# Folding 1/smooth into the values of an attention unit: a GpSimd product and one VectorE product per output

## The reference, cut to what matters

```
core = _gqa(q, k, v).reshape(b, s, nh * d)
...
xout = _gqa(qx, kx, vx).reshape(b, s, nh * d)
cat = jnp.concatenate([core, xout], axis=-1)
catq = _div_clamp_fp8(cat, proj_smooth)
return jnp.einsum('bsi,oi->bso', catq, wproj) * (proj_in_scale * proj_w_scale)
```

## Time and profile before

| | before |
|---|---|
| median of 3 runs | 708.38 us (707.12 to 709.31) |
| span of the profiled execution | 708.0 us |
| PE busy | 623.2 us, 88% |
| DVE busy | 552.2 us, 78% |
| ACT busy | 421.1 us, 59% |
| POOL busy | 274.9 us, 39% |
| mean granted TensorE clock | 0.973 |

### The profile page before, as it was taken

The page is one execution under the profiler, slowest core; times in us unless marked ns, Lnnn a source line. Parts: engine busy times, 40 slices in busy tenths (PEclk is TensorE's granted clock), DMA queues, the critical chain, the costliest instruction groups (busy, mean ns, idle before and its releaser), DMA issues.

```text
span 708.0 us, 13489 instructions
## 1 busy us (share of the span) xinstructions
PE 623.2 (88%) x4521; PEld 496.4 (70%) x4567; DVE 552.2 (78%) x1340; ACT 421.1 (59%) x1371; POOL 274.9 (39%) x371
## 2 busy tenths in 40 slices
PE   4347989988889999999999999999899999999946
PEld 3246767766668777777777877777788787786725
DVE  7997778976677857879788669888864677769698
ACT  4246766755677736566856556657665566673631
POOL 3224663442423563433335544333333256341131
PEclk9987999998999999999999999999999999999987
DMA  8255844743472222322234223422343233320001
GB/s 268 68 181 171 305 127 143 221 156 121 110 229 111 97 98 97 98 98 98 98 112 97 98 82 109 101 97 98 98 146 108 67 124 103 98 31 1 0 1 59
DMA packets 38414, 80.09 MB, mean 113 GB/s; under 512 B 3502, under 2 KB 28746, under 8 KB 33610
## 3 DMA queue, kind: packets, MB, share of 16 engines
q1 hardware_dynamic: 38160, 79.21, 35.5%
q10 hardware_dynamic: 186, 0.02, 0.0%
HBM read 66.62 MB, written 12.60 MB: 112 GB/s over the span
## 4 chain that ended last, share of the span: by engine, by line
PE 57%; DVE 27%; issue 5%; ACT 5%; POOL 3%; DMA 2%; SPq 0%; DVEq 0%; ACTq 0%; POOLq 0%
PE bank L588 12%; PE bank L712 12%; PE bank L692 9%; PE bank L595 6%; PE bank L661 4%; PE bank L736 3%; PE bank L678 2%; DVE Cb L1755 2%; DVE nm L1740 2%; POOL rs L1318 2%; PE bank L693 1%; PE bank L726 1%; DMA WH<-wh_split 1%; DVE Cb L1770 1%; DVE Cb L1771 1%
## 5 line engine op out<-in xcount | busy, mean ns | idle before, releaser
L712 PEld LDWEIGHTS bank<-V,Pt 128*128 128x128 f32 x1024 | 126.7, 192 | 39.3 <-DVE Cb L1755 26.8
L712 PE MATMUL bank<-V,Pt 128*128 128x129 f32 x1024 | 138.0, 278 | 10.5 <-DVE Cb L1755 8.9
L1066 ACT ACTIVATE square<-bank 128x128 bf16<-128x128 f32 x372 | 98.1, 276 | 74.8 <-PE bank L588 45.3
L692 PE MATMUL bank<-QT,KTt 128*128 128x512 f32 x256 | 132.7, 600 | 2.7 <-POOL diag L1342 2.4
L1049 ACT ACTIVATE Pt<-bank 128x512 f32<-128x512 f32 x128 | 76.6, 599 | 74.6 <-remote 49.4
L1740 DVE TENSOR_REDUCE nm<-bank 128x2 f32<-128x512 f32 x128 | 82.1, 683 | 35.8 <-PE bank L678 35.7
L1318 POOL TENSOR_TENSOR rs<-ve,mhalf 128x6 f32<-128x6 f32 x64 | 94.7, 1480 | 5.3
L1342 POOL TENSOR_TENSOR diag<-identb,nm 128x512 bf16<-128x512 bf16 x64 | 67.0, 1047 | 67.3 <-DVE nm L1740 67.2
L588 PE MATMUL bank<-WQ,xq 128*128 128x256 f32 x496 | 79.0, 304 | 9.5 <-DMA WH<-wh_split 3.4
L588 PEld LDWEIGHTS bank<-WQ,xq 128*128 128x128 f32 x496 | 67.0, 196 | 21.9 <-DVE nm L1740 12.0
L1755 DVE SCALAR_TENSOR_TENSOR Cb<-bank,ro,ism 128x128 bf16<-128x128 f32 x256 | 78.1, 347 | 4.5
(11 more groups left out here) (241 smaller groups left out, 1117.2 us busy)
## 6 DMA issues: line engine op xcount, KB each, us to landing
WQ<-wq_split SPq DMA_DIRECT2D x29, 1024.0 KB, 7.7
WH<-wh_split SPq DMA_DIRECT2D x29, 384.0 KB, 8.9
ism<-smooth_inverse SPq DMA_DIRECT2D x32, 256.0 KB, 6.4
wq_split<-stage SPq DMA_DIRECT2D x6, 1024.0 KB, 4.6
wst<-in_L_xattn_wproj SPq DMA_DIRECT2D x16, 256.0 KB, 3.8
wh_split<-stageh SPq DMA_DIRECT2D x6, 384.0 KB, 4.4
wst<-in_L_xattn_wq SPq DMA_DIRECT2D x8, 256.0 KB, 4.7
wst<-in_L_xattn_wqx SPq DMA_DIRECT2D x8, 256.0 KB, 4.7
```

What stands on the lines that cost most here:

```text
L692: nc.tensor.matmul(o[:], KTt[u % 2][:, x, t * P:(t + 1) * P], QT[u % 2][:, x, :], start=True, stop=False)
L712: last = nc.tensor.matmul(o[:, h * (P + 2):h * (P + 2) + P + 1], Pt[:, x, k, h * S + t * P:h * S + (t + 1) * P], V[u % 2][:, x, k, 0:P + 1 ...
L1066: last = A(square[:, t, h], head(t, h), ACT.Square, accum_out=ss[:, t, h:h + 1])
```

## The change

ACT now copies the values to a new tile `Vr`. A new POOL function `scaled_values(u)` makes two products, one for each kind x: values of both key tiles, spread over both heads, times 1/smooth of each head, into a `V` that holds a copy for each head (f32, 512 elements for each partition and product). POOL does it for unit u + 1 right after `half(u + 1)`. PE's `weigh` reads the copy of its head, and waits for the new semaphore `v_scaled` before tile 0 of each kind. An output on DVE is then the reciprocal and one product of two over both heads (256 elements). The wait for `ism` goes from DVE to POOL, and SP's `load_smooth` waits for `v_scaled` of the unit two earlier rather than for its last output.

```diff
-        V = [eb(f"V{i}", [P, 2, NT, P + 4]) for i in range(2)]
+        Vr = [eb(f"Vr{i}", [P, 2, NT, P]) for i in range(2)]
+        V = [eb(f"V{i}", [P, 2, NT, HPG, P + 4]) for i in range(2)]
...
                 if u >= 2:
-                    sp.wait_ge(s["o_evac"], 4 * (u - 1))
+                    sp.wait_ge(s["v_scaled"], 2 * (u - 1))
                 sp.dma_start(ism[:, u % 2], smooth_dram.rearrange("(x f) -> x f", x=2)[:, g * HPG * P:(g + 1) * HPG * P]
...
                 pe.wait_ge(s["exp_done"], 4 * u + 2 * x + 2)
+                if t == 0:
+                    pe.wait_ge(s["v_scaled"], 2 * u + x + 1)
...
-                                                Pt[:, x, k, h * S + t * P:h * S + (t + 1) * P], V[u % 2][:, x, k, 0:P + 1],
+                                                Pt[:, x, k, h * S + t * P:h * S + (t + 1) * P], V[u % 2][:, x, k, h, 0:P + 1],
...
                 if u >= 2 and t == 0:
-                    act.wait_ge(s["pv_done"], 4 * (u - 1))
-                A(V[u % 2][:, :, t, 0:P], QB[2 * t + 1][:].rearrange("p (x j c) -> p x j c", x=2, j=2)[:, :, 1, :], ACT.Copy
+                    act.wait_ge(s["v_scaled"], 2 * (u - 1))
+                A(Vr[u % 2][:, :, t, :], QB[2 * t + 1][:].rearrange("p (x j c) -> p x j c", x=2, j=2)[:, :, 1, :], ACT.Copy
...
+            def scaled_values(u):
+
+                pool.wait_ge(s["v_ready"], 2 * (u + 1))
+                pool.wait_ge(s[f"ism{u % 2}_loaded"], 16 * (u // 2 + 1))
+                if u >= 2:
+                    pool.wait_ge(s["pv_done"], 4 * (u - 1))
+                for x in range(2):
+                    gp.tensor_tensor(V[u % 2][:, x, :, :, 0:P], Vr[u % 2][:, x].unsqueeze(2).to_broadcast([P, NT, HPG, P]),
+                                     ism[:, u % 2, x].rearrange("p (h d) -> p h d", h=HPG).unsqueeze(1)
+                                     .to_broadcast([P, NT, HPG, P]), ALU.mult).then_inc(s["v_scaled"], 1)
...
                     half(u + 1)
+                    scaled_values(u + 1)
                 if u == 2:
                     narrow_parts(5)
                 if u == UNITS - 3:
...
-                if x == 0 and t == 0:
-                    dve.wait_ge(s[f"ism{u % 2}_loaded"], 16 * (u // 2 + 1))
-                    if u >= 2:
-                        dve.wait_ge(s["cT2_done"], u - 1)
+                if x == 0 and t == 0 and u >= 2:
+                    dve.wait_ge(s["cT2_done"], u - 1)
...
-                link(v.reciprocal(ro[:, x, t, :], o[:, 0:HPG * (P + 2)].rearrange("p (h c) -> p h c", h=HPG)[:, :, P]))
-                for h in range(HPG):
-                    last = v.scalar_tensor_tensor(out=c4[:, t, x, h, :], in0=o[:, h * (P + 2):h * (P + 2) + P],
-                                                  scalar=ro[:, x, t, h:h + 1], in1=ism[:, u % 2, x, h * P:(h + 1) * P],
-                                                  op0=ALU.mult, op1=ALU.mult)
-                    if h < HPG - 1:
-                        ch.add(last)
-                last.then_inc(s["o_evac"], 1)
+                heads = o[:, 0:HPG * (P + 2)].rearrange("p (h c) -> p h c", h=HPG)
+                link(v.reciprocal(ro[:, x, t, :], heads[:, :, P]))
+                v.tensor_tensor(c4[:, t, x], heads[:, :, 0:P], ro[:, x, t, :].unsqueeze(2).to_broadcast([P, HPG, P]), ALU.mult
+                                ).then_inc(s["o_evac"], 1)
```

More of the change, by code:

```diff
@@ L1262, in _ @@
             for i in range(2):
-                chain.add(gp.memset(V[i][:, :, :, P:P + 1], 1.0))
+                chain.add(gp.memset(V[i][:].rearrange("p x t h c -> p (x t h) c")[:, :, P:P + 1], 1.0))
             chain.add(gp.memset(OX[:, :, 0:1], NEG_INF))
```

5 lines of the change are left out of this document (3 added, 2 removed).

## The result

| | before | after |
|---|---|---|
| median of 6 runs each | 707.94 us (707.12 to 709.31) | 712.95 us (709.45 to 715.22) |
| ratio, 95% interval | | 1.0070 (1.0046 to 1.0093) |
| span of the profiled execution | 708.0 us | 711.2 us |
| DVE busy | 552.2 us, 78% | 537.8 us, 76% |
| POOL busy | 274.9 us, 39% | 353.5 us, 50% |

The forecast was 706.9 us, with a range of 703.5 to 711.5. The time lies above it. The profiled execution of the changed kernel took 712.99 us, 1.8 us more than its span, and in every other execution for which both are known the time is 1.7 to 1.9 us above the span.

What follows compares the result with a forecast made beforehand. PE, busy 88%, was taken to set the pace. 6.0 us saved on DVE against 2.2 + 0.44 + 0.81 + 1.1 = 4.55 lost takes the span from 708.0 to 706.5; plus 0.4 gives 706.9 us, range 703.5 to 711.5.

Steps and rivals of the forecast that it cites:

- the price: POOL's f32 product of 512 elements with a broadcast: 1.096 us each, 2.19 us a unit, bounds 1.04 and 1.39.
- its faster rival: POOL's products run at 1.04 us and the casts get in first: net -3.6, 704.8 us; chance 0.36.
- the last units: Units 7, 15, 23, 31: PE idles for diag, so its delay counts in full: three at 0.48, one at 0.78, 2.2 us.
- the casts' 1.1: Units 13 and 21: a POOL product may delay DVE's second cast by up to 1.1 us; half taken, 1.1 us for both.
- 13 us for each us of price: How total costs grow with the price of a POOL product; slower by 0.3% begins at 1.37 us.
- Units 27 to 29: Counted among the 25 ordinary units, with slack of 0.94 us or more ahead of scores: no cost.
- What DVE saves: An output's single product takes 0.415 us against 0.610 for the pair; 31 outputs on the chain save 6.0 us.
- Ordinary units hide the products: In 25 of 32 units diag comes 0.48 us late against 0.94 us of slack, so the products cost nothing.
- Unit 3 and unit 30: POOL has little or no idle time ahead of diag, so the products cost 0.44 us in unit 3, 0.81 in 30.
- Elsewhere I found only outputs and maxima: Apart from the casts of units 13 and 21, DVE work beside the products reads PSUM and is free of the lock.
- The median 0.4 us above the span: The runs' median, 708.38 us, lies 0.4 above the span of 708.0; this was added to the predicted span.
- The slow-price rival: Products at 1.39 us, 2.78 a unit, some eight ordinary units run over: 11.3 against 6.0, 713.7 us; chance 0.10.

Runs made afterwards that it cites:

- Experiment 12: The changed kernel with each POOL product multiplying the values by themselves (same tile, flat, 1/smooth left out), in the same place: 705.14 us, ratio 0.9962.
- experiment 11: The kernel before plus idle POOL products behind half: two tiles, two tiles shifted 64 elements, tile and column, one tile 64 elements on: 719.8 us in one run.
- experiment 13: The kernel before plus idle POOL products behind half: one tile with itself 1 to 256 elements on, or two tiles in differing rows: 717.29 us in one run.
- experiment 2: The kernel before plus two idle POOL products of constants behind half in every unit, read by nothing: 717.83 us, ratio 1.0149.
- experiment 4: The changed kernel with the products ahead of half in units 7, 15, 23 and 31 only: 713.71 us, ratio 1.0070.
- experiment 1: The changed kernel with POOL's two products moved ahead of half in all units but the first: 722.4 us, ratio 1.0185.
- experiment 3: The kernel before with the change's shorter output on DVE alone, no POOL products, 1/smooth left out: 701.51 us, ratio 0.9902.
- experiment 5: The changed kernel with the products parted: kind 0 behind half, kind 1 behind the unit's first diag: 708.05 us, ratio 0.9990.
- experiment 8: The changed kernel, products parted, but both ahead of half in units 7, 13, 21, both behind in 0, 12, 20; a wait in 15, 23: 703.46 us, ratio 0.9940.
- experiment 6: The changed kernel with each kind's product moved behind the diag of its kind: 725.81 us, ratio 1.0258.
- experiment 10: The changed kernel with flat product operands, values of both kinds times 1/smooth of both kinds, no broadcasts: 714.05 us, ratio 1.0079.
- experiment 9: The kernel before plus idle POOL products of one tile behind half in four forms (flat, gapped output, broadcast inputs, bf16): 712.95 us in one run.

## Why the prediction was wrong

**The step that failed is the price: "I take 1.096, 2.19 us for a unit".** It measured 2.51 us for the pair, 1.28 by the row of one. Experiment 12 puts a product of 1.04 us in the same place and lands at 0.9962: 2.7 us faster than before by the ratio, 1.9 by the medians, where the forecast had 1.5 and its faster rival, with that price, 3.6. With the price put right the sign and the size of the sum come out, though not all of its parts. The prediction itself said that it was wrong "if the products take over 1.2 us". The rows to choose from were misread: the row of 1.096 is a tile times a column, and that of 1.040 a difference of one tile and itself one element on, both of the cheap kind by experiments 11 and 13. Products of two full streams did stand in the trace of before, as groups whose medians (smallest, median, largest ns; here one of two) say more than the means of 1.34 and 1.35 us, which a single long one draws up:

```profile
L1304 POOL TENSOR_TENSOR tmp<-tmp,vT x4: 1262/1267/1563, 17.5 to 405.9; 128x512 f32<-128x512 f32 x4
```

The Trainium skill ("GPSIMD Engine Reference", 3.1 Elementwise) says that the pace of two-input operations on GpSimd is set by two read streams that take turns. From its 4.497 us for 2048 f32 elements an estimate for 512, in proportion and with no fixed part, is 1.12 us. The measured 1.26 to 1.28 us lie above that estimate, and they decide; no run here shows the port itself.

**What the price alone does to the sum.** By the prediction's own steps a pair of 2.51 us costs the last units 3 x 0.80 + 1.10 = 3.5, unit 3 0.76, unit 30 1.13, and with the casts' 1.1 that is 6.5 against 6.0 saved: 0.5 us slower, not 1.5 faster. Measured are 5.0 us (3.3 to 6.6). So by the sum the price turns the sign, and most of the size lies in what the sum did not have. The "13 us for each us of price" were too few by its own two sums as well: from 4.55 us at 1.096 to 11.3 at 1.39 they rise by 23, and the change against experiment 12 gives 7.6 us for 0.24, some 32. The profile shows three things more:

- **TensorE's clock** (not foreseen). Two stretches of 3.4 us at the lower level, behind 1.89 and 1.70 us of idle time: unit 24's row is 1.60 above the one without it (experiment 12), and the time behind unit 31's first weight load 1.65. Some 3.2 us, more than the 2.0 that the price adds by the sum. That the idle time causes the fall is argued: such idle time came before each of the falls looked at here (2.03 us in experiment 2, 2.76 in 4), but not each such idle time was followed by one, not even 2.78 us in experiment 1. The runs of the change differ by 5.8 us, those of before by 2.2 to 4.6 in the rounds of these experiments; how much of that the clock makes isn't shown.
- **A late `diag` meets other operations of DVE** (wrong). The prediction asked what stands beside the products, and not beside the `diag` that they push back. In unit 3 `diag` takes 1.49 us instead of 1.04, in unit 27 1.50, both beside a two-input operation of DVE, and in 7, 15 and 23 some 1.23 beside the uint16 operation. In unit 3:

```profile
125.41 0.95 DVE L1593 TENSOR_TENSOR tmp<-tmp 128x512 f32<-128x512 f32 x1
125.77 1.49 POOL L1356 TENSOR_TENSOR diag<-identb,nm 128x512 bf16<-128x512 bf16 x1
```

- **Units 27 to 29** (wrong). They were counted as ordinary, with 0.94 us of slack. POOL's gap there was 1.56 us, not 1.71, and `diag` is stretched in 27 and 28: 0.51, 0.21 and 0.05 us, 0.8 together.

Row by row against experiment 3, the products cost 1.46 us in unit 3, 4.2 in 7, 15, 23 and 31, 1.14 in 30, 1.4 in 13 and 21, 0.8 in 27 to 29, and 2.6 in the two rows in which the clock was low (24 and behind 31): 11.6 us, where the spans of the two kernels differ by 11.2 (711.2 and 700.0).

**What DVE saves** (right): 0.424 us against the 0.415 of the nearest row, and 6.7 us of time against 6.0 (experiment 3).

**Ordinary units hide the products** (right, but barely): 0.20 us of slack are left where the sum had some 0.46, and in experiment 2, where no output is shortened, their rows are 0.00 to 0.01.

**The last units pay in full** (right in kind): 1.89 us of PE's idle time in 15 and 23, 1.70 in 31, against the 1.3 foretold; the price gives 0.32 of the difference, and `diag` beside the uint16 operation of DVE 0.19 in the first two. **Unit 3 and unit 30**: their rows are +1.11 and +0.75, and without products -0.35 and -0.39 (experiment 3), so the products cost 1.46 and 1.14 us. The sum had 0.44 and 0.81, and has 0.76 and 1.13 at the measured price: right for unit 30, too little for unit 3, where the longer `diag` adds 0.45 (together 1.21; PE was idle for 1.23).

**The casts of 13 and 21** (right in size by luck, wrong in the way). The 1.1 us for both stood for a product that gets in between `half` and the second cast. In the change none does: the cast takes 0.48 us, where experiment 3, without products, has 0.49, and the products begin behind it. What is caught stands a turn earlier. The products make `diag` of unit 12 late, and beside it `fq`, an operation of two elements for each partition, takes 0.90 us instead of 0.17; the maxima behind it are late, and PE's weight load for the next `project` waits for them for 1.13 us instead of 0.78. The timeline of units 12 and 13, before:

```profile
305.94 0.17 DVE L1486 TENSOR_SCALAR fq<-fq 128x2 f32<-128x2 f32 x1
...
308.08 1.01 PEld L588 LDWEIGHTS bank<-WQ,xq 128*128 128x128 f32 x8 [0.78 <-DVE nm L1740]
```

The same of the changed kernel:

```profile
303.87 1.04 POOL L1356 TENSOR_TENSOR diag<-identb,nm 128x512 bf16<-128x512 bf16 x1
...
304.04 0.90 DVE L1502 TENSOR_SCALAR fq<-fq 128x2 f32<-128x2 f32 x1
...
306.90 1.01 PEld L589 LDWEIGHTS bank<-WQ,xq 128*128 128x128 f32 x8 [1.13 <-DVE nm L1756]
...
318.67 0.48 DVE L1749 CAST KTh<-KTt 128x256 bf16<-128x256 f32 x1
...
318.97 2.57 POOL L1337 TENSOR_TENSOR V<-Vr,ism 128x512 f32<-128x512 f32 x2
```

The rows are +0.29 each, where the shorter output alone has -0.41: 0.70 a unit. `fq` goes with them in the other kernels, 1.20 us and +0.6 in the parted one, 0.90 and +0.30 in experiment 8. A product does get ahead of the cast where no shorter output moves the casts earlier: +1.42 in unit 21 of experiment 2. So "Elsewhere I found only outputs and maxima" missed what the delayed `diag` meets, and experiments 1, 4, 5 and 6 show how little it holds at other places; the prediction had named it as a sign of being wrong, "if other DVE operations than the two casts are caught by the lock".

The lock itself is as the Trainium skill has it ("SBUF — State Buffer", Who interferes with whom): casts, `tensor_scalar` and operations with two SBUF inputs can be shut out for as long as GpSimd's operation lasts. The traces agree: a cast ends 0.14 us and a `tensor_scalar` 0.29 us behind the product that it met (1.32 and 1.55 us, experiments 1 and 6), and two operations with two inputs take 3.32 us beside products that take 3.31 (experiment 4).

**The median 0.4 us above the span** (wrong): it is 1.8. The profiled execution of before, 708.0 of span, so belongs to some 709.8 us, an estimate, and is one of its slowest; a difference from it should have been taken off its own time, or the 1.5 us off the median, 706.9 all the same.

**The slow-price rival** (713.7 at 1.39 us) came out near the time, but not by its way: its price was too high, and of the ordinary units that it had running over only 27 to 29 did.

**Open**: why two streams within 4 elements are cheap, and why three groups of before, one of them of two different tiles, read 1.09 us; the clock's fall after one idle time and not after the next.

## What to carry to other kernels

A price for work that moves to another engine is taken from a row with the same operands, not the same shape: two full streams, a stream and a column, and a tile with itself are three things, and the median of a group tells more than its mean. Then look at what the target engine shares with its neighbours: a gap in POOL's queue is only free if DVE isn't on casts, `tensor_scalar` or two-input operations on SBUF at that time, and it can pay to wait until it has done. Ask the same of every POOL operation that the new work pushes back. And where PE stands idle in dense work as long as here (1.5 to 2.8 us), count that the clock may fall behind it; each fall cost another 1.6 us.

## What the runs showed of the hardware that was not expected

- On GpSimd a product of 512 f32 elements takes 1.04 us with a column, with the same tile, or with the same tile up to 4 elements on, and 1.27 to 1.30 us with an address 16 or more elements away, with or without broadcasts (experiments 10, 11 and 13); with the same tile and broadcasts on both 1.16 (experiment 9), the mean of the two.
- A DVE `TENSOR_SCALAR` of two f32 elements for each partition, 0.17 us before, took 0.90 us beside `diag` in the changed kernel and 1.20 beside a product in the parted one.
- TensorE's granted clock fell to 0.50 to 0.53 for 3.4 us at a time, within 1.4 us of the end of idle times of 1.5 to 2.8 us in the middle of dense work, at a cost of 1.6 us (units 13 and 21 of experiment 2; the spans of the change and experiment 10), and no fall came behind some idle times of the same length (1.89 us in unit 15 of the change, 2.02 us in unit 21 of experiment 11, 2.78 us in unit 14's turn of experiment 1).
